# Two buffers for transposed input and values, loop bodies of two batches, and a new order of work in a fused attention and mixture layer

## What is computed

```
for each of 32 batches x [256, 128]:
    n  = layernorm(x)
    Q, K, V = n W_Q + b_Q, n W_K + b_K, n W_V + b_V      # 16 heads of 64
    out = softmax(Q K^T / 8) V, projected by W_O, + b_O
    x1 = x + layernorm(out)
    n1 = layernorm(x1)
    gate = softmax(n1 G^T)                               # 8 experts
    z = n1 W^T + (1/16) sum_e gate_e * V_e (U_e n1)      # rank 16
    x  = x1 + layernorm(z)
```

## Time and profile before

| | |
|---|---|
| median of 3 runs | 1090.09 us (1090.06 to 1090.18) |
| profiled execution | 1091.16 us, its span 1089.3 us |
| PE busy | 1021.8 us, 94% |
| DVE, ACT, POOL busy | 905.9, 917.7, 800.1 us |
| mean granted TensorE clock | 0.979 |

### The profile page before, as it was taken

One profiled execution on the slowest core, in us unless ns is written; L12 is line 12 of the kernel. 1 busy time (PEld: TensorE's weight loads), 2 busy tenths in 40 slices (PEclk: granted clock), 3 DMA queues, 4 the chain that ended last, 5 costly groups with the idle time before them and its releaser, 6 DMA issues.

```text
span 1089.3 us, 28626 instructions
## 1 busy us (share of the span) xinstructions
PE 1021.8 (94%) x8550; PEld 780.2 (72%) x8550; DVE 905.9 (83%) x1630; ACT 917.7 (84%) x3207; POOL 800.1 (73%) x778
## 2 busy tenths in 40 slices
PE   8889999999999999999999999999999999999974
PEld 7767777777777777677777777777767777777743
DVE  6888888888888888888888888888888888888841
ACT  4888888889888888888888989888988888898932
POOL 3676777787777788777778777778877777877741
PEclk9899999999999999999999999999999999999977
DMA  7364566556556556556655655755655665565570
GB/s 239 85 149 108 133 152 144 121 130 142 122 136 159 127 121 146 125 122 153 147 122 125 146 121 132 159 131 122 142 129 121 149 152 122 121 149 123 128 164 11
DMA packets 59219, 145.21 MB, mean 133 GB/s; under 512 B 17216, under 2 KB 25920, under 8 KB 59200
## 3 DMA queue, kind: packets, MB, share of 16 engines
q1 hardware_dynamic: 59200, 144.99, 57.7%
HBM read 6.50 MB, written 4.19 MB: 10 GB/s over the span
## 4 chain that ended last, share of the span: by engine, by line
PE 87%; ACT 4%; issue 3%; DVE 3%; POOL 2%; ACTq 0%; POOLq 0%; DVEq 0%
PE o_ps L460 22%; PE st_ps L438 18%; PE extra_ps L476 8%; PE qk_ps L404 8%; PE qk_ps L406 5%; PE qk_ps L405 5%; PE extra_ps L334 5%; PE extra_ps L418 4%; PE extra_ps L420 3%; PE extra_ps L419 3%; PE extra_ps L497 2%; PE extra_ps L510 2%; ACT v_sb L739 2%; ACT xt_hi L705 1%; PE extra_ps L512 1%
## 5 line engine op out<-in xcount | busy, mean ns | idle before, releaser
L1516 POOL TENSOR_TENSOR probs<-probs,inv_sum 128x1024 f32<-128x1024 f32 x256 | 486.3, 1900 | 201.4 <-DVE inv_sum L1097 201.2
L724 ACT ACTIVATE probs<-st_ps,neg_max 128x256 f32<-128x256 f32 x1024 | 477.9, 483 | 32.5 <-DVE neg_max L1089 30.2
L1089 DVE TENSOR_REDUCE neg_max<-st_ps 128x4 f32<-128x1024 f32 x256 | 310.0, 1211 | 44.7 <-PE st_ps L438 35.5
L1105 DVE STREAM_TRANSPOSE probs_b<-probs 128x1024 f32<-128x1024 f32 x256 | 313.4, 1225 | 26.8 <-POOL probs L1516 26.8
L460 PE MATMUL o_ps<-probs_t,v_sb 128*64 128x256 f32 x2048 | 253.7, 390 | 7.7 <-DVE o_lo L1113 4.3
L724 ACT ACTIVATION_READ_ACCUMULATOR probs<-st_ps,neg_max 128x1 f32 x1024 | 217.9, 213 | 0.0
L460 PEld LDWEIGHTS o_ps<-probs_t,v_sb 128*64 128x64 f32 x2048 | 136.8, 138 | 89.4 <-issue 16.0
L710 ACT CAST qk_hi<-qk_ps 128x512 fp32r<-128x512 f32 x256 | 153.5, 599 | 29.7 <-PE qk_ps L406 26.1
L438 PE MATMUL st_ps<-qk_hi 64*128 64x256 f32 x1024 | 171.9, 332 | 3.8 <-POOL qk_lo L1510 1.5
L438 PE MATMUL st_ps<-qk_lo,qk_hi 64*128 64x256 f32 x1024 | 145.2, 280 | 0.0
L1510 POOL TENSOR_TENSOR qk_lo<-qk_full,qk_hi 128x512 fp32r<-128x512 f32 x96 | 123.5, 1286 | 28.1 <-ACT qk_hi L710 14.6
(11 more groups left out here) (132 smaller groups left out, 1988.6 us busy)
## 6 DMA issues: line engine op xcount, KB each, us to landing
probs_t<-probs_b SPq DMA_DIRECT2D x1024, 128.0 KB, 2.4
out<-x_all SPq DMA_DIRECT2D x31, 128.0 KB, 1.9
x_all<-in_x SPq DMA_DIRECT2D x1, 3840.0 KB, 17.3
probs_b<-in_w_v SPq DMA_DIRECT2D x1, 512.0 KB, 4.9
probs_b<-in_w_o SPq DMA_DIRECT2D x1, 512.0 KB, 6.8
probs_b<-in_w_q SPq DMA_DIRECT2D x1, 384.0 KB, 5.3
probs_b<-in_w_k SPq DMA_DIRECT2D x1, 384.0 KB, 5.9
x_all<-in_x SPq DMA_DIRECT2D x2, 128.0 KB, 3.5
```

Source lines behind the costliest of these rows:

```text
L724: last = nc.scalar.activation(probs[n][:, h, j, :], st_ps[p % 2][:, (2 * h + j) * T:(2 * h + j + 1) * T], ACT.Exp, bias=neg_max[n][:, h, j ...
L1089: nc.vector.tensor_reduce(neg_max[p % N_PROBS][:, :, :].rearrange("p h j -> p (h j)"), st_ps[p % 2][:, :].rearrange("p (j s) -> p j s", j= ...
L1105: nc.vector.transpose(probs_b[chunk % 2][:, :, :, 2 * NT * n:2 * NT * (n + 1), :].rearrange("p i t n q -> p n t i q"), probs[p % N_PROBS][ ...
L1516: nc.gpsimd.tensor_tensor(probs[n][:, :, :, :].rearrange("p h j s -> p (h j) s"), probs[n][:, :, :, :].rearrange("p h j s -> p (h j) s"), ...
```

## The change

- `xt_hi`, `xt_lo` and `v_sb` become two buffers each, taken in turn by the parity of the batch. The waits of `xt_high` and `copy_v` look one batch further back.
- `run` makes one loop turn of two batches, so that the parity is fixed in each half. The first turn of each loop (DVE: of batch 5, others: of batch 3) stands unrolled where the count would be odd.
- `POOL_LO` goes from the pairs 1, 4, 6 to the pairs 1, 5. The three `qk_full` buffers become one.
- Small tiles share homes: `x1t` is `yt`, `ut` is `u`, `squares` are these two, and `mean_ident` and `neg_mean_w` (used at the start only) lie in `probs_t[1]`.
- The order on all engines is a new one.

The helpers, cut:

```diff
-POOL_LO = (1, 4, 6,)
+POOL_LO = (1, 5,)
...
-            with engine.Fori(0, high - low) as step:
-                body(step + low)
+            with engine.Fori(0, (high - low) // 2) as step:
+                for n in range(2):
+                    body(2 * step + (low + n), (low + n) % 2)
...
-            def xt_high(b):
+            def xt_high(b, turn):
                 act.wait_ge(x_transposed, b + 1)
-                after(act, qk_projected, PAIRS * b)
-                after(act, v_projected[3], b)
-                nc.scalar.activation(xt_hi[:, :], extra_ps[:, 0:T], ACT.Identity,
+                after(act, qk_projected, PAIRS * (b - 1))
+                after(act, v_projected[3], b - 1)
+                nc.scalar.activation(xt_hi[turn][:, :], extra_ps[:, 0:T], ACT.Identity,
...
-                sem, count = lo_written(b - 1, p)
-                after(act, sem, count)
-                nc.scalar.copy(qk_full_sb[p][:, :], qk_ps[p % 2][:, :]).then_inc(qk_full_ready, 1)
+                k = POOL_LO.index(p)
+                after(act, *(lo_written(b, POOL_LO[k - 1]) if k else lo_written(b - 1, POOL_LO[-1])))
+                nc.scalar.copy(qk_full_sb[:, :], qk_ps[p % 2][:, :]).then_inc(qk_full_ready, 1)
...
-                after(act, o_projected, PAIRS * (b - 1) + (half + 1) * (PAIRS // 2))
-                nc.scalar.copy(v_sb[:, quarter % 2, half * HALF:(half + 1) * HALF],
+                after(act, o_projected, PAIRS * (b - 2) + (half + 1) * (PAIRS // 2))
+                nc.scalar.copy(v_sb[turn][:, quarter % 2, half * HALF:(half + 1) * HALF],
...
-                after(act, y_transposed, b)
+                after(act, z_projected, b)
...
-                after(dve, u_transposed, b)
+                after(dve, variance_ready[LN_Z], b)
```

More of the change, by code:

```diff
@@ new lines, in _ @@
+            output_projection(0, free=(v_copied[3], 2))
+            project_qk(2, 4, 0)
+            project_v(2, 0, 0, free=(yt_ready, 1))
+            scores(2, 2)
+            transpose_y(0, free=(v_copied[0], 3))
+            scores(2, 3)
+            probs_v(1, 0, 1)
+            probs_v(1, 1, 1)
+            transpose_x1(0, free=(x1_ready, 1))
+            project_qk(2, 5, 0)
+            project_tg(0, free=(x1t_ready, 1))
+            project_qk(2, 6, 0)
+            scores(2, 4)
+            probs_v(1, 2, 1)
@@ new lines, in _ @@
+            probs_v(1, 3, 1)
+            transpose_u(0, free=(u_ready, 1))
+            project_qk(2, 7, 0)
+            project_v(2, 1, 0, free=(ut_ready, 1))
+            scores(2, 5)
+            project_z(0, free=(v_copied[1], 3))
+            probs_v(1, 4, 1)
+            probs_v(1, 5, 1)
+            project_v(2, 2, 0, free=(z_copied, 1))
+            scores(2, 6)
+            def body(i, r):
+                transpose_xn(i, free=(v_copied[2], i))
+                probs_v(i - 2, 6, r)
+                probs_v(i - 2, 7, r)
+                project_qk(i, 0, r)
+                project_v(i - 1, 3, 1 - r, free=(xt_lo_ready, i + 1))
+                project_qk(i, 1, r)
+                scores(i - 1, 7)
@@ L889, in _ @@
[L889 to L897 removed]
+            qk_hi(2, 3)
+            exponentials(2, 1, 1)
+            copy_yt(0)
+            exponentials(2, 1, 0)
+            copy_v(2, 0, 0)
+            square_y(0)
+            qk_hi(2, 4)
+            exponentials(2, 2, 1)
@@ L954, in body @@
-                attention_hi(i - 1, 3)
-            run(act, 3, B, body)
+            body(3, 1)
+            run(act, 4, B, body)
+            exponentials(31, 5, 1)
             exponentials(31, 6, 0)
@@ L1280, in _ @@
             aggregate_x1(0)
-            invert_sum(2, 1)
-            transpose_blocks(2, 0)
+            qk_lo(2, 4)
+            attention_lo(1, 0)
+            gate_max(0)
+            scale_gate_max(0)
+            invert_sum(2, 2)
             row_max(2, 3)
+            apply_gate(0)
             transpose_blocks(2, 1)
+            transpose_blocks(2, 2)
+            invert_sum(2, 3)
+            row_max(2, 4)
             attention_lo(1, 1)
-            gate_max(0)
-            invert_sum(2, 2)
@@ L1299, in _ @@
-            transpose_blocks(2, 3)
-            qk_lo(2, 7)
-            def body(i):
-                spread_x(i)
-                row_max(i - 3, 6)
-                invert_sum(i - 3, 5)
-                transpose_blocks(i - 3, 4)
-                xt_low(i - 2)
-                attention_lo(i - 4, 3)
+            invert_sum(2, 5)
+            transpose_blocks(2, 4)
+            attention_lo(1, 3)
+            qk_lo(3, 0)
+            def body(i, r):
+                spread_x(i)
+                invert_sum(i - 3, 6)
```

719 lines of the change are left out of this document (337 added, 382 removed).

## The result

The changed kernel takes 1011.07 us (median of 4 runs, 1010.16 to 1011.72) beside 1090.13 us: ratio 0.9273, interval 0.9257 to 0.9289.

The account below looks back on a forecast made before the run. TensorE, busy 94%, was taken to bound the kernel. From the profiled 1091.16 us, loops save 56.0, start 3.6 and end 0.5, giving 1031.1, as median 1030; own range 1022 to 1038, with rival 1 and part of rival 2 1021 to 1052.

Parts of the forecast that it names:

- Start and end: Unrolled batches around the loops: start 3.6 us shorter, end 0.5 us shorter, each with bounds for idle time.
- The prediction's own sign: Stated test: the forecast is wrong if the turn exceeds 30.6 us a batch or the ends change by over 8 us.
- floor: Loop turn per batch with waits gone and fewer changes of product kind, no loss: 29.83 us, from 32.13.
- The walk's losses: Stepping once through the new turn: 0.19 us at copy_yt and 0.15 at copy_ut lost, 0.34 in all.
- three waits: TensorE's loop waits for copy_v, xt_low and copy_yt, 0.83, 0.50 and 0.06 us a turn, would go: 1.39 us.
- Double buffers: Next x is prepared while old buffers are read; the copy_v stall goes if timely, and xt_low is hidden.
- Remainders: One pair moves from POOL to DVE: ACT loses 0.62 us a turn, DVE gains 0.67; neither sets the turn by its sum.
- Rival 1: VectorE falls behind in the loop, one us a turn: +26 us, 1056 us; half of that, 1043; chance 0.17.
- Code: Two-batch turns have twice the instructions; refetching them was costed at nothing.
- Rival 2: Loop branch misses on ScalarE or VectorE, 14 stalls of 2.4 us, 34 us: 1047 to 1064 us; chance 0.08.
- Rival 4: TensorE refetches its own longer loop: slower from 4.3 us a turn, at 6 us a turn 1114 us; chance 0.03.
- Rival 3: The new order doesn't remove the 0.19 us per change of product kind, only waits go: 31.1 a turn, 1056; chance 0.04.

Follow-up runs that it names:

- a_split: Kernel after with the pair 1 projection put between its two adjacent score groups, two more changes of product kind a turn; 1027.06 us, ratio 0.9425.
- b_buffers_pad: Kernel before with new buffers, shared homes and two-batch loops in its old order, plus 160 fulfilled waits ahead of ScalarE's work; 1085.63 us, ratio 0.9961.
- a_dve_tight: Kernel after with three extra unused bn_stats on VectorE each turn, right ahead of apply_gate; 1022.36 us, ratio 0.9382.
- a_pad16: Kernel after with 16 already fulfilled waits (8 instructions) ahead of ScalarE's work, nothing else; 1044.16 us, ratio 0.9583.
- b_buffers: Kernel before with new buffers, shared homes and two-batch loops, in its old order with three pairs on GpSimd; 1139.34 us, ratio 1.0447.
- b_new_start: Start of the kernel after, then the old order's two-batch loops and end with GpSimd pairs 1 and 5; 1133.06 us, ratio 1.0408.
- b_new_start_pad: New start before old-order two-batch loops and end, GpSimd pairs 1 and 5, plus 168 fulfilled waits ahead of ScalarE's work; 1088.73 us, ratio 0.9997.

## Why the prediction was wrong, point by point

**What fell: the step "Start and end".** It said of the start's 10.5 us of idle PE that "the new order may win or lose some; bounds -8 and +4, I take -0.9: -3.6 in all". Measured: -13.3. Idle went from 10.5 to 6.5, but busy from 96.1 to 86.8, of which only 2.7 was moved. The other 6.6 is near half of the 15.1 us for which PE was busy in the three slow stretches (5.51, 6.16 and 3.40), what the same work would save at the higher level; that is a sum, not an experiment. The term did not hold it at all, since it counted idle time alone. What moved both was in the diff and not walked: the new start transposes x of batches 1 and 2 earlier, and the engines fill sooner. Undoing that gave back 6.1 and 4.7 us. The prediction's own sign, ends that change by over 8 us, is what came. The end was taken at -0.5 and came to -4.3, past its bound of -4; products without use in the old end win 2.4, so more than half of a gain of this size is to be had from the clock alone. The granted clock did rise from 0.71 to 0.80 in the new end, but how its 4.3 us divide between clock and order was not isolated.

**The range failed with it.** Its low end, 1021, held a turn of 29.9 and the start and end near their taken values. The prediction's own bounds, 29.83 a turn, -2.7 - 8 and -4, add up to 1091.16 - 66.7 - 10.7 - 4 - 1.07 = 1008.7, which holds the time. Unknown terms that I had bounded were then not kept in the range.

**The turn was right in its mechanism and 0.2 us too long.** 29.83 as floor and 30.2 taken, 30.00 measured; the 0.2 a turn make 5.9 of the 19 us missed, the start 9.7 and the end 3.8 (19.4 in the profiled executions). The walk's losses of 0.34 came at less than half. `copy_yt` cost 0.12 and, a turn earlier, 0.17 for 0.19; behind `copy_ut` the quarter starts 0.12 us after the product before it, so 0.15 was not lost.

```profile
493.76 0.28 PE L407 MATMUL qk_ps<-xt_hi,wk_lo 128*128 128x256 f32 x1
494.05 0.48 PE L419 MATMUL extra_ps<-wv_hi,xt_hi 128*128 128x512 f32 x1
...
506.73 0.28 PE L407 MATMUL qk_ps<-xt_hi,wk_lo 128*128 128x256 f32 x1
506.85 0.41 PE L419 MATMUL extra_ps<-wv_hi,xt_hi 128*128 128x512 f32 x1
```

29.83 and the mean of the two, 0.15, are 29.98. The floor is confirmed by this total and, for the price of a change, by `a_split`; its three waits are gone from the list but for single ones outside the loop.

**Double buffers** let the order be and win next to nothing by themselves (`b_buffers_pad`, 0.1 us a turn). The prediction put the three waits, 1.39 us, down to the buffers and order together and did not say which.

**Remainders.** The groups answer to the earlier trace rows, by shape, from the kernel after:

```profile
L1083 DVE TENSOR_TENSOR qk_lo<-qk_ps,qk_hi 128x512 fp32r<-128x512 f32 x192 | 126.8, 660 | 2.3 <-ACT qk_hi L712 2.2
...
L719 ACT COPY qk_full<-qk_ps 128x512 f32<-128x512 f32 x64 | 37.9, 592 | 0.1
```

64 copies and 192 remainders, as counted. *Rival 1* (VectorE behind) is wrong: it waits 1.1 us a turn for the rstd, where I had 0.8. But `a_dve_tight` shows the walk right on where it is tight: 0.1 us of spare at `transpose_u` by the walk, 0.14 measured.

**Code.** Costed at nothing: right for this kernel, 14 and 16 packets. *Rival 2* had a chance of 0.08, and its price, 34 us, was met by `a_pad16` (33.1) and exceeded by `b_buffers` (53.7 over its padded version). The nearness of 33.1 is partly luck: the 2.4 us were the time of a data transfer of 128 KB. In the kernel after the rival stayed away by fewer than 8 instructions; the chance was too low for what was known.

The compiled programs show why. TensorE's is 229 KB and the other four engines' are 122 KB together, which is what q8 and q14 carried (0.23 and 0.12 MB): each program once. TensorE's 229 KB are 3582 instructions, so one is 64 bytes, a packet of q14 (8 KB) has 128 and one of q8 (16 KB) 256. ScalarE's loop, from its head to its branch, counted from 0 in its own program:

| kernel | head and branch of the loop | q14 packets |
|---|---|---|
| after | 431, 710 | 16 |
| `b_new_start` | 439, 718 | 80 |
| `a_pad16` | 439, 718 | 80 |
| `b_buffers` | 447, 730 | 80 |
| `b_new_start_pad` | 523, 802 | 16 |
| `b_buffers_pad` | 527, 810 | 16 |

Every `ACTIVATION_READ_ACCUMULATOR`, a row of its own in the trace, is an instruction of its own here. The expectations above had left these out and so had 203 for 279 instructions and 207 for 283; a shift of 8 is the same in both counts, but their loop that lies in two blocks of 128 does not stand. If some 50 to 57 instructions lie ahead of the count, the three loops with 80 packets touch three blocks of 256 and the other three two (by blocks of 128 it is four and three, which fits as well). That is an inference from six kernels.

The Trainium skill ("Runtime: NRT & Kernel Launch", section "Instruction fetch mechanics") has blocks of 256 instructions and a window of two of them, and a taken branch out of this window waits for a fetch. That fits all six kernels, with the stall of 2.0 to 2.7 us at the branch. The prediction took from it the size alone, a loop that fits in 512 instructions; 279 do, and yet lie across three blocks when they start late enough in the first. *Rival 4* is wrong: with 1,141 instructions in its loop TensorE has 14 packets in all.

**Rival 3** (the change of kind isn't what goes) is wrong: it gave 31.1 a turn, and `a_split` paid for its two changes.

## What to carry to other kernels

Price the unrolled start and end like a turn, by walking them; a term bounded by 12 us and then taken at -0.9 is no estimate, and what it is bounded by belongs in the range. A gain in the start counts only if the loop behind takes the work over; here the old one did not. Idle time that a clock answers is dearer than it looks, so busy time of a start or an end is a term too. Where a hardware loop is lengthened, look at the instruction queues of the new profile and at each engine's first instruction behind the branch: some idle instructions ahead of the loop cost 33 us here, and gave back 54 in another version.

## What the runs showed of the hardware

- Eight instructions of shift ahead of ScalarE's loop made 64 more packets of code and 33.1 us in 14 turns, the engine idle for 2.0 to 2.7 us at the branch. TensorE's loop, four times as long as ScalarE's, had nothing of the kind.
- A change between split projections and scores cost TensorE 0.19 us one way and 0.20 the other, booked as busy: the two starts at the change are 0.21 to 0.22 us apart instead of 0.12.
- The granted clock fell to the lower level in or behind idle stretches of TensorE in the start and the end. Filling them won 2.4 us in the old end, and nothing that could be measured in the old start.
